# Attention on one core: the mask added with the row extreme on VectorE, and the heads' turns and copies in another order

## What is computed

```python
q = (inputs @ Wq + bq).reshape(bs, n, N_HEADS, HEAD_DIM)
k = (inputs @ Wk + bk).reshape(bs, n, N_HEADS, HEAD_DIM)
v = (inputs @ Wv + bv).reshape(bs, n, N_HEADS, HEAD_DIM)
logits = jnp.einsum('bqhd,bkhd->bhqk', q, k) / np.sqrt(HEAD_DIM)
mask = (adj > 0)[:, None, :, :]
logits = jnp.where(mask, logits, NEG_INF)
attn = jax.nn.softmax(logits, axis=-1)
out = jnp.einsum('bhqk,bkhd->bqhd', attn, v).reshape(bs, n, EMBED_DIM)
return jax.nn.relu(out @ Wo + bo)
```

## Time and profile before

| | |
|---|---|
| time, median of 3 runs | 3022.4 us (3019.73 to 3022.41) |
| the profiled execution | 3024.76 us, its span 3023.0 us |
| busy in the span | PE 2772.3 us (92%), PEld 2452.8 (81%), DVE 1674.8 (55%), ACT 1784.0 (59%), POOL 1503.2 (50%) |
| mean granted clock of PE | 0.980 |
| row maxima (line 421) | 256 reductions, 157.3 us busy, 677 ns each |
| covers (line 583) | 256 matmuls of 512 columns, 379 ns each |

### The profile page before, as it was taken

The page is one execution under the profiler, slowest core; times in us unless marked ns, Lnnn a source line. Parts: engine busy times, 40 slices in busy tenths (PEclk is TensorE's granted clock), DMA queues, the critical chain, the costliest instruction groups (busy, mean ns, idle before and its releaser), DMA issues. The chain is left out here.

```text
span 3023.0 us, 113835 instructions
## 1 busy us (share of the span) xinstructions
PE 2772.3 (92%) x43200; PEld 2452.8 (81%) x43200; DVE 1674.8 (55%) x5581; ACT 1784.0 (59%) x4834; POOL 1503.2 (50%) x2681
## 2 busy tenths in 40 slices
PE   6999999978888888769999999999999999999957
PEld 5777777667777777759889898999999899999956
DVE  6887888634444444446666664544444445454558
ACT  4666666644444444437667665666666577767723
POOL 5777777510000000046666665555555566666644
PEclk9999999999999999979999999999999999999979
DMA  2111111000000000020000011000000100000002
GB/s 88 43 35 35 35 43 35 13 11 12 13 13 12 13 13 13 13 73 26 26 21 26 24 30 48 9 9 7 9 9 7 34 9 9 9 7 9 9 21 90
DMA packets 110487, 72.32 MB, mean 24 GB/s; under 512 B 51424, under 2 KB 109280, under 8 KB 110432
## 3 DMA queue, kind: packets, MB, share of 16 engines
q1 hardware_dynamic: 96464, 58.93, 6.7%
q10 hardware_dynamic: 13968, 12.72, 1.4%
HBM read 50.63 MB, written 20.97 MB: 24 GB/s over the span
## 5 line engine op out<-in xcount | busy, mean ns | idle before, releaser
L1464 PE MATMUL g_F<-g_w,g_act 128*128 128x256 f32 x3072 | 698.0, 380 | 0.0
L1464 PEld LDWEIGHTS g_F<-g_w,g_act 128*128 128x128 f32 x3072 | 578.4, 191 | 75.1
L1447 PE MATMUL g_H<-g_hT_upper,g_w_upper 128*128 128x256 f32 x1536 | 442.6, 288 | 0.0
L1447 PE MATMUL g_H<-g_hT_upper,g_w_rest 128*128 128x256 f32 x1536 | 435.0, 283 | 0.0
L1447 PE MATMUL g_H<-g_hT_rest,g_w_upper 128*128 128x256 f32 x1536 | 434.7, 283 | 0.0
L744 POOL COPY l_xt<-seq 128x64 f32 x256 | 60.9, 238 | 597.5 <-PE l_O L755 595.8
L328 ACT ACTIVATE a_probs<-a_S,a_nmax 128x256 f32<-128x256 f32 x512 | 236.7, 480 | 123.2 <-DVE a_nmax L421 89.8
L1104 ACT ACTIVATE g_act<-g_H,g_small 128x256 f32<-128x256 f32 x768 | 291.4, 490 | 6.0 <-PE g_H L1447 4.8
L1447 PEld LDWEIGHTS g_H<-g_hT_upper,g_w_upper 128*128 128x128 f32 x1536 | 294.5, 192 | 0.1
L1447 PEld LDWEIGHTS g_H<-g_hT_upper,g_w_rest 128*128 128x128 f32 x1536 | 294.5, 192 | 0.0
L1447 PEld LDWEIGHTS g_H<-g_hT_rest,g_w_upper 128*128 128x128 f32 x1536 | 294.5, 192 | 0.0
(11 more groups left out here) (207 smaller groups left out, 7244.3 us busy)
## 6 DMA issues: line engine op xcount, KB each, us to landing
gmask<-masks ACTq DMA_DIRECT2D x97, 128.0 KB, 2.0
x<-in_x_dram SPq DMA_DIRECT2D x32, 256.0 KB, 3.1
a_adj<-in_adj_dram SPq DMA_DIRECT2D x32, 256.0 KB, 2.7
hidden<-l_hs SPq DMA_DIRECT2D x512, 16.0 KB, 1.4
g_hs<-hidden SPq DMA_DIRECT2D x32, 256.0 KB, 2.7
out_dram<-q_res SPq DMA_DIRECT2D x32, 256.0 KB, 2.1
g_w<-in_L_gnn_W_dram SPq DMA_DIRECT2D x6, 1024.0 KB, 6.2
masks<-gmask SPq DMA_DIRECT2D x32, 128.0 KB, 1.7
```

The costliest lines, as they stand in the source:

```text
L1447: last = pe.matmul(hidden_bank[m // 2][:, m % 2 * N:(m % 2 + 1) * N], w[:, c, m * P:(m + 1) * P], x[:, c, :], start=(c == 0 and k == 0), s ...
L1464: last = pe.matmul(ff_bank[:, it * D:(it + 1) * D], act1[:, m, it * P:(it + 1) * P], w2[:, m, :], start=(m == 0 and it == 0), stop=(m == M ...
```

## The change

- The mask is no longer put into the banks by PE: `cover` is gone, and `scores` opens the accumulation itself.
- The scaled queries and their bias are negated, so the bank holds negated scores, and the mask is 0 or +1e30. `smallest` (DVE) takes the place of `largest`: for each head and row tile it adds the mask to the bank in place and takes the row minimum; ACT's exponent has a scale of -1.
- `reciprocals(b)` follows `k_out(b + 1)` at the end of DVE's graph b; it was the first step of graph b + 1.
- The copies of heads 1 and 5 go from DVE to ACT: `EARLY` copies are those of heads 0 and 4 (DVE), `LATE` ones those of 1, 2, 3, 5, 6 and 7 (ACT).
- DVE: `heads_out` and `v_out` stand ahead of `moments1`; the copy of head 4 follows `q_out`.
- PE: the turns keep their places between `values`, `queries` and `keys`, without covers between them, and wait for the copies by the new counts.
- POOL's `masks` waits for the row minima, not for the scores.

```diff
--- before.py
+++ after.py
@@ -141,6 +141,7 @@
         tiny_done, spread_done = sem("tiny_done"), sem("spread_done")
         proj_ps, gated_done, x_done = sem("proj_ps"), sem("gated_done"), sem("x_done")
 
+        EARLY, LATE = 2, 6
         passed, pool_passed = sem("passed"), sem("pool_passed")
         bias_done = sem("bias_done")
 
@@ -242,9 +243,9 @@
 
                 def masks(b, i):
 
-                    after(pool, scores_ps, (b - 1) * H)
+                    after(pool, max_done, (b - 1) * H)
                     alone(pool, adj_in, b * 16 + 16, pool_passed)
-                    pool.tensor_scalar(mask[i][:, :], adj[:, :, :].rearrange("p t n -> p (t n)"), 0.0, MASKED,
+                    pool.tensor_scalar(mask[i][:, :], adj[:, :, :].rearrange("p t n -> p (t n)"), 0.0, -MASKED,
                                        ALU.is_le, ALU.mult).then_inc(mask_done, 1)
 
                 def gmasks(b):
@@ -326,7 +327,8 @@
                     after(act, turned_ps, b * H + h + 1 - PROBS)
                     for it in range(NT):
                         last = act.activation(probs[h % PROBS][:, it, :], score_bank[h % HG][:, it * N:(it + 1) * N],
-                                              ACT.Exp, bias=nmax[:, h, it:it + 1], accum_out=den[:, h, it:it + 1])
+                                              ACT.Exp, bias=nmax[:, h, it:it + 1], scale=-1.0,
+                                              accum_out=den[:, h, it:it + 1])
                     last.then_inc(probs_done, 1)
 
                 def late_out(b, h):
@@ -352,6 +354,7 @@
                     if exists(b - 1):
                         rden_out(b - 1)
                     exponent(b, 2)
+                    late_out(b, 1)
                     exponent(b, 3)
                     late_out(b, 2)
                     if exists(b + 1):
@@ -359,8 +362,10 @@
                     if exists(b - 2):
                         xn2T_out(b - 2)
                     late_out(b, 3)
-                    for h in range(HG, H):
+                    for h in range(HG, H - 1):
                         exponent(b, h)
+                    late_out(b, 5)
+                    exponent(b, H - 1)
                     late_out(b, 6)
                     late_out(b, 7)
 
@@ -415,11 +420,17 @@
                     dve.tensor_tensor(v[:, :, :], in_bank[:, :].rearrange("p (t d) -> p t d", t=NT),
                                       bv_row[:, :].unsqueeze(1).broadcast_to((P, NT, D)), ALU.add).then_inc(v_done, 1)
 
-                def largest(b, h):
-
-                    dve.wait_ge(scores_ps, b * H + h + 1)
-                    dve.tensor_reduce(nmax[:, h, :], score_bank[h % HG][:, :].rearrange("p (t k) -> p t k", t=NT), AX.X,
-                                      ALU.max, negate=True).then_inc(max_done, 1)
+                def smallest(b, h, i):
+
+                    if h == 0:
+                        dve.wait_ge(mask_done, b + 1)
+                    alone(dve, scores_ps, b * H + h + 1, passed)
+                    for it in range(NT):
+                        part = score_bank[h % HG][:, it * N:(it + 1) * N]
+                        last = dve.tensor_tensor_reduce(out=part, in0=part, in1=mask[i][:, it * N:(it + 1) * N], scale=1.0,
+                                                        scalar=3.0e38, op0=ALU.add, op1=ALU.min,
+                                                        accum_out=nmax[:, h, it:it + 1])
+                    last.then_inc(max_done, 1)
 
                 def early_out(b, h):
 
@@ -463,39 +474,36 @@
                     last.then_inc(mv2_done, 1)
 
                 def graph(b, i):
+                    for h in range(HG):
+                        smallest(b, h, i)
+                    early_out(b, 0)
                     if exists(b - 1):
-                        reciprocals(b - 1)
-                    for h in range(HG):
-                        largest(b, h)
-                    early_out(b, 0)
+                        heads_out(b - 1)
+                    v_out(b)
                     if exists(b + 2):
                         moments1(b + 2)
-                    if exists(b - 1):
-                        heads_out(b - 1)
-                    early_out(b, 1)
-                    v_out(b)
                     if exists(b + 1):
                         xnT_rest_out(b + 1)
                     for h in range(HG, H):
-                        largest(b, h)
+                        smallest(b, h, i)
                     if exists(b - 1):
                         gate(b - 1)
-                    early_out(b, 4)
                     if exists(b + 1):
                         q_out(b + 1)
+                    early_out(b, 4)
                     if exists(b - 1):
                         residual(b - 1)
-                    early_out(b, 5)
                     if exists(b + 1):
                         k_out(b + 1)
+                    reciprocals(b)
                     if exists(b - 1):
                         moments2(b - 1)
 
                 dve.tensor_copy(ident_int[:, :], t.ident[:, :]).then_inc(ident_done, 1)
                 moments1(0)
                 dve.wait_ge(rows_in, 4 * 16)
-                dve.memset(qscale[:, :], HD ** -0.5)
-                dve.tensor_scalar(bqs_col[:, :], bq_col[:, :], HD ** -0.5, None, ALU.mult).then_inc(bqs_done, 1)
+                dve.memset(qscale[:, :], -HD ** -0.5)
+                dve.tensor_scalar(bqs_col[:, :], bq_col[:, :], -HD ** -0.5, None, ALU.mult).then_inc(bqs_done, 1)
                 moments1(1)
                 dve.wait_ge(weights_in, 4 * 16)
                 for upper, w in zip(w_upper, (wq, wk, wv)):
@@ -510,7 +518,6 @@
                 q_out(0)
                 k_out(0)
                 walk(dve, graph)
-                reciprocals(B - 1)
                 heads_out(B - 1)
                 gate(B - 1)
                 residual(B - 1)
@@ -576,28 +583,22 @@
                                             [w[2][:, c, :] for w in (w_upper, w_rest)], c == 0, c == KC - 1)
                     last.then_inc(v_ps, 1)
 
-                def cover(b, h, i):
-
-                    if h == 0:
-                        pe.wait_ge(mask_done, b + 1)
-                    pe.matmul(score_bank[h % HG][:, :], t.identb[:, :], mask[i][:, :], start=True, stop=False, skip_group_check=True)
-
                 def scores(b, g):
                     pe.wait_ge(k_done, b * KC + g + 1)
                     for it in range(NT):
                         for j in range(HG):
                             o = HD * j
                             last = pe.matmul(score_bank[j][:, it * N:(it + 1) * N], qT[o:o + HD, g, it * P:(it + 1) * P],
-                                             kT[o:o + HD, g, :], start=False, stop=True, skip_group_check=True)
+                                             kT[o:o + HD, g, :], start=True, stop=True, skip_group_check=True)
                             if it == NT - 1:
                                 last.then_inc(scores_ps, 1)
 
                 def turn_probs(b, h):
                     pe.wait_ge(probs_done, b * H + h + 1)
-                    if h % HG < 2:
-                        after(pe, late_done, b * (H // 2) + h // HG * 2 + h % 2 - 1)
+                    if h % HG == 2:
+                        pe.wait_ge(early_done, b * EARLY + h // HG + 1)
                     else:
-                        pe.wait_ge(early_done, b * (H // 2) + h // HG * 2 + h % 2 + 1)
+                        after(pe, late_done, b * LATE + {0: -1, 1: 0, 3: 1, 4: 2, 5: 3, 7: 4}[h])
                     for kt in range(NT):
                         for it in range(NT):
                             last = pe.transpose(turn_bank[h % 2][:, kt * N + it * P:kt * N + (it + 1) * P],
@@ -606,8 +607,8 @@
 
                 def weigh(b):
 
-                    pe.wait_ge(late_done, (b + 1) * (H // 2))
-                    pe.wait_ge(early_done, (b + 1) * (H // 2))
+                    pe.wait_ge(late_done, (b + 1) * LATE)
+                    pe.wait_ge(early_done, (b + 1) * EARLY)
                     pe.wait_ge(v_done, b + 1)
                     after(pe, gated_done, b)
                     for g in range(KC):
@@ -638,36 +639,31 @@
                     scores(b, 0)
                     if exists(b - 1):
                         weigh(b - 1)
-                    for h in range(2):
-                        turn_probs(b, h)
-                        cover(b, h + HG, i)
+                    turn_probs(b, 0)
+                    turn_probs(b, 1)
                     values(b)
                     turn_probs(b, 2)
-                    cover(b, 2 + HG, i)
                     if exists(b - 2):
                         turn_xn2(b - 2)
                     if exists(b + 1):
                         turn_xn(b + 1)
                     turn_probs(b, 3)
-                    cover(b, 3 + HG, i)
                     scores(b, 1)
                     if exists(b - 1):
                         project(b - 1)
-                    for j in range(HG):
```

(17 more changed lines are left out.)

## The result

The changed kernel takes 3049.4 us (median of four runs, 3047.7 to 3050.7), the kernel before 3022.4 (3019.7 to 3023.1). The ratio is 1.0090, with an interval of 1.0074 to 1.0106: slower by 27 us, where 3031 - 3022 = 9 were forecast. The profiled execution took 3048.9, its span 3047.1.

What follows compares the result with a forecast made beforehand. The attention stage was taken as bound by what PE waits for on DVE and ACT, not its busy share. +0.93 and -0.64 a graph over 31 graphs, +9.0 less about 0.3, gave 3031 us; range 3020 to 3045.

Steps and rivals of the forecast that it cites:

- Turn 6 waits for copy 4: Second half: PE's turn 6 waits for DVE's copy of head 4 behind `q_out`, delaying `keys`; the half changes by +0.93.
- the copy doesn't hold PE: Rival, second half: turn 6 finds its bank free, only gains stay, -0.73 a graph, 3000 us, faster; chance 12%.
- The earlier `v_out`: First half: `v_out` runs 0.20 after turn 2 instead of 0.61, `turn_xn` at 7.33 instead of 7.75; the half changes by -0.64.
- The end without a cover: End of the first half: `scores` follows turn 3 after 0.53 instead of 0.75, the cover being gone.
- the price of the row minimum: DVE, both halves: two minima a head at 0.345 each, 0.69 a head instead of 0.61; first exponent 0.09 later.
- 0.04 (my estimate): Second half, DVE: the new separate wait instruction puts some 0.04 us ahead of the first minimum.
- The "milder" rival: Minimum written into the bank takes 0.40 each: +0.11 in each half, +7 in all, 3038; within the forecast, no own chance.
- Costed at nothing: Two late copies on ACT (0.5 each), the sign flip, earlier reciprocals, GpSimd's mask wait and SP's loads: no cost or gain.
- The clock's rival: PE idles more and its granted clock falls to 0.50 in every other graph: +23, 3054 us; chance 4%.
- that of a minimum of 0.61: Rival: the minimum written into the bank takes 0.61 each, `q_out` and `v_out` wait, +2.7 a graph, 3106 us; chance 5%.
- The halves cancel: Rival: first half ends at PE's own pace and `keys` takes 1.42, a graph changes by +0.1, 3025 us; chance 27%.

Runs made afterwards that it cites:

- experiment 1: The changed kernel with DVE's copy of head 4 put back ahead of `q_out`: 3018.0 us, ratio 0.9977 to the kernel before.
- experiment 2: The kernel before with only the copy of head 4 moved behind `q_out`: 3058.9 us, ratio 1.0114.
- experiment 4: The kernel before with only `heads_out`, the copy of head 1 and `v_out` moved ahead of `moments1`: 3013.7 us, ratio 0.9967.
- experiment 5: The changed kernel with masked scores of heads 4 to 7 written to SBUF, where the exponent reads them, not into the bank: 3050.9 us, ratio 1.0088.
- experiment 8: On top of experiment 1, ACT's `xn2T_out` moved ahead of `xnT_out`: 3018.7 us, beside 3018.0 without it.
- experiment 3: The kernel before with the mask moved from PE to DVE, no covers, order and copies as before: 3039.6 us, ratio 1.0054.
- experiment 11: Kernel before with negated queries, heads 3 and 7 masked on DVE, others covered, `v_out` ahead of `moments1`, `xn2T_out` first, covers 0 to 2 moved: 3005.8 us, ratio 0.9942.
- experiment 12: On top of experiment 11, `xnT_rest_out` moved between the minima of heads 5 and 6: 3008.5 us, ratio 0.9948.
- experiment 7: The changed kernel with `reciprocals` put back as the first step of DVE's next graph: 3050.9 us, beside 3049.4.
- experiment 9: On top of experiment 4, cover 7 moved ahead of `turn_xn` and the next graph's cover 0 behind turn 7: 3012.3 us, ratio 0.9961.
- experiment 10: On top of experiment 4, cover 7 moved ahead of `turn_xn` and `xn2T_out` ahead of `xnT_out` on ACT: 3015.1 us, ratio 0.9973.
- experiment 6: The changed kernel with one more semaphore increment of DVE ahead of each head's minima: 3057.5 us, ratio 1.0108.

## Why the prediction was off

The sign and the mechanism were right; the size, 9 us instead of 27, was not. The term that was mis-sized is what stands between `scores` and the first exponent of each half: the row minimum and the wait and increment ahead of it. Point by point:

- **Turn 6 waits for copy 4: right.** From `q_out` on, the second half ran as worked out: copy 4 0.91 behind it (0.91), turn 6 1.74 (1.69), `keys` 2.12 (2.12), turn 7 3.62 (3.60), `scores` 4.36 (4.34). Experiments 1 and 2 confirm it from both sides: 8.85 instead of 9.85, and 9.84 instead of 8.63. The rival "the copy doesn't hold PE" is out.
- **The earlier `v_out`: right** (0.20 behind turn 2; experiment 4 gains 0.36 a graph by it alone, on the old kernel). **The end without a cover: right** (0.53).
- **The failed step is the price of the row minimum.** "I take 0.345, since it is the same operation" and "0.04 (my estimate)" for the separate wait, which no row of the kernel before shows. The same operation with its output in the bank costs more: 0.38 between starts and 0.14 for the read, by experiment 5. From the first minimum to the exponent 0.90 (second half) and 0.99 (first half) were measured, for 0.82 and 0.84; experiment 5 accounts for 0.09, in the second half, and what makes the first half's another 0.06 is open. Ahead of the first minimum stands 0.16 for 0.04 in the second half, and 0.12 for nothing in the first, where the prediction had no such term. In the table below the error is complete at exponent 0 or turn 4 and then stays the same to the end.

| us after `scores` | predicted | measured | error |
|---|---|---|---|
| second half: minimum | 1.20 | 1.32 | 0.12 |
| exponent 4 | 2.02 | 2.22 | 0.20 |
| turn 4 | 3.09 | 3.37 | 0.28 |
| `q_out` | 5.22 | 5.48 | 0.26 |
| next `scores` | 9.56 | 9.84 | 0.28 |
| first half: minimum | 1.44 | 1.56 | 0.12 |
| exponent 0 | 2.28 | 2.55 | 0.27 |
| turn 2 | 6.30 | 6.55 | 0.25 |
| next `scores` | 8.32 | 8.58 | 0.26 |

The errors are 0.28 + 0.26 = 0.54 a graph, 31 x 0.54 = 17 us: 3031 + 17 = 3048, and 3049.4 were measured. By place, 0.24 are ahead of the minima, some 0.23 between the first minimum and the exponent, and 0.08 at turn 4. Of turn 4's 0.28 the last 0.08, from exponent 4 to turn 4, is not the minimum's: from the second exponent's start to the turn are 0.68 in the changed kernel and in experiments 1 and 8, built on it, but 0.61 or 0.62 before and in experiments 3, 11 and 12, which have masks on DVE but keep the order of the copies and the counts that the turns wait for. Which of these two it is was not tried.

- **The range.** The "milder" rival, 0.40 each, had the right direction and was priced at +7, to 3038. The upper end, 3045, lay 4 us short: it gave the unknown write into the bank its due, but the separate wait and increment had no bound of their own, and in the first half no term at all. The 0.12 and 0.12 that were missing there are 31 x 0.24 = 7 us.
- The Trainium skill's estimate (VectorE: DVE Perf Modes, the section on the TRN2 errata; 0.39 us for 256 elements out of PSUM) was nearer to the 0.38 measured than the row of the graph network was. But its table has the price for an output in SBUF, and with that the instruction takes 0.35 here (experiment 5), so that the agreement is luck.
- **Costed at nothing: mostly right.** The reciprocals (experiment 7). The late copies on ACT were tried only together with the rest; experiment 1 with them has a first half of 8.58, experiment 4 without them and with covers 8.57. Of the covers, experiment 9 shows that the one behind turn 7 lies there for nothing, and experiment 10 that the one of head 7 doesn't. The clock's rival is out (1.00), and that of a minimum of 0.61 too.
- **The halves cancel** (3025) fails by the second half's +1.22. Without the copy behind `q_out` the halves more than cancel: experiment 1 is that kernel, at 3018.0.

The account of the change in parts, by the halves: copy 4 behind `q_out` +1.00 a graph (31 us, experiment 1). All the rest together gives 17.66 - 17.80 = -0.14 by the halves of experiment 1, or -6 us by its times. In it is the mask on DVE, which by itself cost 16 us (experiment 3), and the order of `v_out`, which by itself gave 10 (experiment 4); the sum of these two, +6, isn't the -6 measured. The likely reason is that they act on each other: with minima on DVE `v_out` is later still (0.87 behind turn 2), so that putting it forward is worth more, 3039.6 - 3018.0 = 22 us together with the copies that went to ACT (3018.0 is experiment 1, which has all three). How the 22 divide between order and copies was not tried.

## What to carry to other kernels

When an engine's queue is reordered, write the timetable of the other engine that waits for it from the first wait on, and ask for each pair that changes places which of the two has the longer chain behind it: here a 0.9 us instruction moved ahead of a 0.7 us copy cost 31 us, and no busy share names it. Price a replaced instruction by a row with the same source and the same destination, and count the waits and increments that stand alone in front of it, in every place where a burst begins. Work on PE that fills its waits is nearly free, and moving it to the engine that PE waits for makes the kernel slower; what paid was to move only two heads of eight, one of whose covers stood where PE had no wait (8 us beyond the order of `v_out`, together with a change of order on ACT).

## What the runs showed of the hardware

- The minimum instruction of 256 f32 elements out of a bank: 0.345 between starts and 0.08 for the accumulator read with its output in SBUF, 0.38 and 0.14 with its output in the same bank (experiment 5).
- The exponent of 256 elements with its accumulator read: 0.45 to 0.47 between starts out of a bank, 0.49 to 0.51 out of SBUF (experiment 5).
- A semaphore increment that is an instruction of its own costs 0.09 to 0.10 us ahead of the first minimum of a burst, and nothing within it (experiment 6).
- A second cover behind turn 7 moved `scores` by its whole 0.22 (experiment 9): the 0.31 between a cover and `scores` is no idle time.
- PE's clock stayed at 1.00 with PE busy for 88% of the attention stage.
